# Pair 0's first layer by batches and in an order of its own, the last pair's gates by halves, the slot rows squared on VectorE

## The reference

```python
xn = _layernorm(x)
s = _L0_attn_ref(xn, ...)      # s = xn Wspin + b; e = s WJ; P = softmax(e s^T / sqrt(128))
                               # tanh(beta * (s + mean(s) Wglobal + P s))
g = _silu(_L0_ffn_ref(xn, ...))  # r = sigmoid(xr Wr); k = relu(xk Wk)^2; r * (k Wv); xr, xk mix each token with the one before
x = x + s * g
xn = _layernorm(x)
s = _L1_attn_ref(xn, ...)      # 16-head retention with decay mask, |scores| denominators, RMS norm, gate, Wo
g = _silu(_L1_ffn_ref(xn, ...))  # soft mixture of 8 experts with 64 slots each; slot rows are RMS-normalised once
x = x + s * g
```

## Time and profile before

| what | us |
|---|---|
| median of 3 runs | 1065.32 (1065.32 to 1065.45) |
| the profiled execution, its own time | 1065.09 |
| its span | 1063.3 |
| TensorE busy | 1046.6 (98%) |
| VectorE busy | 918.8 (86%) |
| ScalarE busy | 810.7 (76%) |
| GpSimd busy | 414.3 (39%) |
| TensorE busy in the first 32 us | 23.51 |
| TensorE busy from 1052 to 1060.5 us | 5.86 |

### The profile page before, as it was taken

How to read it: one execution, slowest core, us unless ns; L and a number is a source line. 1 busy time by engine, 2 the same in 40 slices (tenths; PEclk the granted TensorE clock), 3 DMA queues, 4 the chain that set the end, 5 groups by cost and what they waited for, 6 DMA issues and landing times.

```text
span 1063.3 us, 27317 instructions
## 1 busy us (share of the span) xinstructions
PE 1046.6 (98%) x10266; PEld 824.9 (78%) x10266; DVE 918.8 (86%) x1818; ACT 810.7 (76%) x1434; POOL 414.3 (39%) x555
## 2 busy tenths in 40 slices
PE   7999999999999999999999999999999999999997
PEld 4578787877878778787787878778787787877866
DVE  4888988888998888898888988889988889988775
ACT  4577878778787787877778787886877878787775
POOL 2532434334353433534334443343534325343240
PEclk9999999999999999999999999999999999999999
DMA  6000000000000000000000000000000000000000
GB/s 263 12 11 2 2 22 2 21 2 11 12 2 21 2 15 8 2 21 2 21 2 2 22 2 21 2 11 13 2 21 2 21 2 1 23 1 11 2 12 10
DMA packets 18463, 16.85 MB, mean 16 GB/s; under 512 B 800, under 2 KB 17440, under 8 KB 18080
## 3 DMA queue, kind: packets, MB, share of 16 engines
q1 hardware_dynamic: 18336, 15.12, 4.4%
HBM read 10.93 MB, written 4.19 MB: 14 GB/s over the span
## 4 chain that ended last, share of the span: by engine, by line
PE 94%; DVE 2%; issue 1%; ACT 1%; POOL 0%; DVEq 0%; ACTq 0%; POOLq 0%
PE bank L1031 13%; PE bank L987 11%; PE bank L977 11%; PE bank_s L1008 7%; PE bank L997 6%; PE bank L968 5%; PE bank L938 5%; PE bank L833 3%; PE bank L931 3%; PE bank L864 3%; PE bank L960 3%; PE bank L918 3%; PE bank_s L1011 3%; PE bank L884 3%; PE bank L1038 3%; PE bank L1046 2%
## 5 line engine op out<-in xcount | busy, mean ns | idle before, releaser
L326 POOL TENSOR_TENSOR ret_abs<-ret_abs 128x512 f32<-128x512 f32 x128 | 182.3, 1427 | 250.8 <-ACT ret_abs L479 250.6
L659 DVE TENSOR_TENSOR ret<-bank_s,k_sb 128x1536 f32<-128x1536 f32 x128 | 223.7, 1748 | 29.8 <-PE bank_s L1011 20.2
L479 ACT ACTIVATE ret_abs<-ret 128x1536 f32<-128x1536 f32 x128 | 189.6, 1481 | 26.5 <-DVE ret L659 26.5
L987 PEld LDWEIGHTS bank<-w_sb,hact 128*128 128x128 f32 x1024 | 127.9, 191 | 18.0 <-issue 7.8
L987 PE MATMUL bank<-w_sb,hact 128*128 128x128 f32 x1024 | 138.6, 278 | 0.0
L333 POOL TENSOR_SCALAR dT<-dT,drec 128x256 f32<-128x256 f32 x128 | 67.0, 541 | 170.2 <-DVE drec L723 170.2
L977 PE MATMUL bank<-slotsT,w_sb 128*128 128x128 f32 x1024 | 130.1, 275 | 0.4 <-ACT slotsT L469 0.4
L977 PEld LDWEIGHTS bank<-slotsT,w_sb 128*128 128x128 f32 x1024 | 123.2, 192 | 1.7 <-ACT slotsT L469 0.8
L474 ACT ACTIVATE hact<-hact 128x512 f32<-128x512 f32 x128 | 80.2, 628 | 52.1 <-DVE hact L728 51.7
L1031 PE MATMUL bank<-ret,vrow 128*32 128x256 f32 (+1 forms) x2048 | 108.2, 329 | 0.3 <-POOL ret_abs L326 0.3
L1031 PEld LDWEIGHTS bank<-ret,vrow 128*32 128x32 f32 x2048 | 59.9, 109 | 42.0 <-issue 2.5
(11 more groups left out here) (145 smaller groups left out, 2274.2 us busy)
## 6 DMA issues: line engine op xcount, KB each, us to landing
x_sb<-x SPq DMA_DIRECT2D x16, 256.0 KB, 2.7
w_sb<-w SPq DMA_DIRECT2D x2, 2048.0 KB, 14.0
out<-attn SPq DMA_DIRECT2D x16, 256.0 KB, 2.3
v_sb<-vectors SPq DMA_DIRECT2D x1, 705.0 KB, 7.3
k_sb<-consts SPq DMA_DIRECT2D x1, 538.0 KB, 6.1
w_sb<-weights SPq DMA_DIRECT2D x1, 512.0 KB, 4.4
w_sb<-weights SPq DMA_DIRECT2D x1, 320.0 KB, 3.2
slot_sb<-slot_rows SPq DMA_DIRECT2D x1, 256.0 KB, 3.3
```

The costliest lines, as they stand in the source:

```text
L326: pool.tensor_tensor(both[:, :, P:SEQ], both[:, :, P:SEQ], both[:, :, SEQ:3 * P], ALU.add)\
L479: act.activation(ret_abs[:, q % MR], ret[:, q % MR], ACT.Abs).then_inc(ready["ab"].sem, 1)
L659: dve.tensor_tensor(ret[:, q % MR], bank_s[:, :, 0:3 * P], causal.unsqueeze(1).broadcast_to([P, Q, 3 * P]), ALU.mult)\
L987: ins = pe.matmul(bank[:, i * C:(i + 1) * C], hact[:, i, c], w2_sb[:, e, c], start=(c == 0), stop=(c == HC - 1))
```

## The change

Three things are changed. First, `steps_of` takes the lists `FIRST` and `LAST`: step 0 runs in the order of `FIRST` on TensorE, VectorE and ScalarE, and in the last step the tasks named in `LAST` run behind the others, in its order. Second, in pair 0 the tasks `xnT`, `xnTc`, `s`, `sT`, `e`, `eTc`, `local`, `field`, `sp`, `prod`, `x1`, `xn2T` and `xn2Tc` are cut into one part for each batch, with a semaphore `half[...]` for the first; the second batch's results go to the retention's banks `bank_s`, as does `r`. In the last pair `zt`, `zg`, `sg`, `x2` and the store are cut in the same way. Third, VectorE squares the slot rows with one product and one reduction right behind `xn`, waiting for their own load alone, and scales them right behind `mix`. The fillers behind `slots_across` go from eight to four.

```diff
+FIRST = {
+    "PE": [("xnT", 0), ("s", 0), ("e", 0), ("k", 0), ("score", 0), ("global", 0), ("score", 1), ("r", 0), ("PT", 0),
+           ("srow", 0), ("PT", 1), ("v", 0), ("local", 0)],
+    "DVE": [("stat", 0), ("xn", 0), ("mix", 0), ("gbias", 0), ("smax", 0), ("smax", 1), ("ka", 0), ("srec", 0), ("srowc", 0),
+            ("rv", 0), ("field", 0), ("rvg", 0), ("field", 1), ("prod", 0), ("x1", 0), ("prod", 1), ("x1", 1), ("stat2", 0)],
+    "ACT": [("xnTc", 0), ("sT", 0), ("eTc", 0), ("kr", 0), ("sgT", 0), ("P", 0), ("P", 1), ("PTc", 0), ("PTc", 1), ("tr", 0),
+            ("tv", 0), ("sp", 0)]}
+LAST = {
+    "DVE": [("z", 0), ("gated", 0), ("gated", 1), ("z", 1), ("zg", 0), ("attn", 0), ("sg", 0), ("x2", 0), ("zg", 1),
+            ("attn", 1), ("sg", 1), ("x2", 1)],
+    "PE": [("out", 0), ("o", 0), ("out", 1), ("o", 1)]}
+
+EARLY_BANK = {"xnT": 1, "s": 2, "e": 3, "r": 0, "local": 1}
...
-        slot_sq = dT[:, 0, 0, 0:C]
+        slot_sq = d[:].rearrange("p j s -> p (j s)")[:, 0:4 * C].rearrange("p (j c) -> p j c", j=4)
...
+            def in_order(step):
+                under_way = [(name, k, step - age) for name, k, age in order if 0 <= step - age < pairs]
+                if step == 0 and first:
+                    return [(name, k, 0) for name, k in first]
+                if step == pairs + ages - 1 and last:
+                    return [u for u in under_way if u[0] not in {name for name, _ in last}] + [(*u, pairs - 1) for u in last]
+                return under_way
...
-            sp.dma_start(slot_sb[:], slot_rows).then_inc(loaded.sem, 16)
+            sp.dma_start(slot_sb[:], slot_rows).then_inc(rows_in.sem, 16)
...
-            store(pairs - 1)
-            sp.wait_ge(*stored(pairs - 1))
+            rows = out[bass.ds((pairs - 1) * TOK, TOK), :].rearrange("(j p) c -> p j c", p=P)
+            for b in range(2):
+                sp.wait_ge(*(ready["x2"](pairs - 1) if b else half["x2"](0)))
+                sp.dma_start(rows[:, 2 * b:2 * b + 2], attn[:, 2 * b:2 * b + 2]).then_inc(stored.sem, 16)
+            sp.wait_ge(stored.sem, 16 * (pairs + 1))
...
             def slot_norms():
-                pool.wait_ge(loaded.sem, 64)
...
+            def batches(name, done, p, copy):
+
+                for b in range(2):
+                    act.wait_ge(*(filled if b else half)[name](p))
+                    bank = early_bank(name) if b else banks[BANK[name, 0]][:, 0:SEQ]
+                    copy(b, bank).then_inc((ready if b else half)[done].sem, 1)
...
-            def slot_squares():
-                act.wait_ge(loaded.sem, 64)
-                for j in range(4):
-                    if j:
-                        act.wait_ge(ready["slot_ready"].sem, j)
-                    act.activation(slot_sq, slot_sb[:, j], ACT.Square, accum_out=slot_n[:, 0, j:j + 1])\
-                        .then_inc(ready["slot_ready" if j < 3 else "slot_sqs"].sem, 1)
...
+            def slot_squares():
+                dve.wait_ge(rows_in.sem, 16)
+                dve.tensor_tensor(slot_sq, slot_sb[:], slot_sb[:], ALU.mult).then_inc(ready["slot_sq"].sem, 1)
+                dve.wait_ge(*ready["slot_sq"](0))
+                dve.tensor_reduce(slot_n[:, 0], slot_sq, X, ALU.add).then_inc(ready["slot_sqs"].sem, 1)
...
+            def turn_batches(bank, other, src, name):
+                for b in range(2):
+                    pe.wait_ge(*(ready if b else half)[name](0))
+                    for i in range(2):
+                        ins = pe.transpose((bank, other)[b][:, i * P:(i + 1) * P], src[:, 2 * b + i], ident)
+                    ins.then_inc((filled if b else half)[name + "T"].sem, 1)
...
             def s(p, par, k):
+                if p == 0:
+                    for b, bank in enumerate((claim("s", p), early_bank("s"))):
+                        pe.wait_ge(*(ready if b else half)["xnTc"](p))
+                        pe.matmul(bank[:, 0:SEQ], W["spin"], xnT[:, b, 1:SEQ + 1], start=True, stop=True)\
+                          .then_inc((filled if b else half)["s"].sem, 1)
+                    return
...
-                turn_over(8)
+                turn_over(4)
...
```

More of the change, by code:

```diff
@@ L216, in build @@
             ("eoc", E // 2), ("crec", 2), ("z", 2), ("zt", 1), ("zg", 1), ("sg", 1), ("x2", 1))}
+        half = {name: signal(f"half_{name}") for name in (
+            "xn", "xnT", "xnTc", "s", "sT", "e", "eTc", "local", "field", "sp", "prod", "x1", "xn2", "xn2T", "zt", "zg", "sg", "x2")}
         passed = {name: signal(f"passed_{name}") for name in ("vector", "gpsimd")}
@@ L224, in since, with steps_of @@
                 eng.wait_ge(*signal(p, k))
-        def steps_of(tasks, order, between=()):
-            for step in range(pairs + ages):
-                for name, k, age in order:
-                    p = step - age
-                    if 0 <= p < pairs:
-                        tasks[name](p, p % 2, k)
-                        if p == 0 and (name, k) in between:
-                            between[name, k]()
+        def steps_of(tasks, order, first=(), last=(), between=()):
+            def in_order(step):
[5 more added lines that the diff above has]
+                return under_way
+            for step in range(pairs + ages):
+                for name, k, p in in_order(step):
+                    tasks[name](p, p % 2, k)
+                    if p == 0 and (name, k) in between:
+                        between[name, k]()
         block = ctx.enter_context(nc.Block())
@@ L384, in eTc @@
             def eTc(p, par, k):
+                if p == 0:
+                    batches("e", "eTc", p, lambda b, bank: act.activation(eT[:, b * SEQ:(b + 1) * SEQ], bank, ACT.Copy))
+                    return
                 bank = bank_of("e", p)
@@ L424, in xn2Tc @@
             def xn2Tc(p, par, k):
+                if p == 0:
+                    for b in range(2):
+                        act.wait_ge(*(filled if b else half)["xn2T"](p))
+                        bank = early_bank("xnT") if b else banks[BANK["xn2T", 0]][:, 0:SEQ]
+                        ins = act.activation(xn2T[:, b], bank, ACT.Copy)
+                    ins.then_inc(ready["xn2Tc"].sem, 1)
+                    return
                 bank = bank_of("xn2T", p)
@@ L551, in xn_ @@
                                             ALU.subtract, ALU.mult)
+                    if p == 0 and j == 1:
+                        ins.then_inc(half["xn"].sem, 1)
                 ins.then_inc(ready["xn"].sem, 1)
@@ L583, in field @@
             def field(p, par, k):
+                if p == 0:
+                    dve.wait_ge(*ready["srowc"](p))
+                    dve.wait_ge(*ready["srec"](p))
+                    dve.wait_ge(*(filled if k else half)["local"](p))
+                    bank = bank_s[:, EARLY_BANK["local"]] if k else banks[BANK["local", 0]]
+                    for i in range(2):
+                        j = 2 * k + i
+                        ins = dve.scalar_tensor_tensor(out=spin[:, j], in0=bank[:, i * P:(i + 1) * P], scalar=srec[:, j:j + 1],
+                                                       in1=srow[:, j], op0=ALU.mult, op1=ALU.add)
+                    ins.then_inc((ready if k else half)["field"].sem, 1)
+                    return
                 bank = bank_of("local", p)
@@ L850, in e @@
             def e(p, par, k):
+                if p == 0:
+                    for b, bank in enumerate((claim("e", p), early_bank("e"))):
+                        pe.wait_ge(*(ready if b else half)["sT"](p))
+                        pe.matmul(bank[:, 0:SEQ], W["J"], sT[:, b], start=True, stop=True)\
+                          .then_inc((filled if b else half)["e"].sem, 1)
+                    return
                 pe.wait_ge(*ready["sT"](p))
@@ L859, in score @@
             def score(p, par, b):
-                pe.wait_ge(*ready["eTc"](p))
+                pe.wait_ge(*(half if p == 0 and b == 0 else ready)["eTc"](p))
                 bank = claim("score", p, b)
@@ L878, in local @@
                 pe.wait_ge(*ready["srowc"](p))
-                pe.wait_ge(*ready["PTc"](p, 1))
+                if p:
+                    pe.wait_ge(*ready["PTc"](p, 1))
                 bank = claim("local", p)
@@ L882, in local @@
                     b, i = divmod(j, 2)
+                    if p == 0 and i == 0:
+                        pe.wait_ge(*ready["PTc"](p, b))
+                    to = early_bank("local")[:, i * P:(i + 1) * P] if p == 0 and b else bank[:, j * P:(j + 1) * P]
                     for m in range(2):
-                        ins = pe.matmul(bank[:, j * P:(j + 1) * P], probT[:, b, m, i * P:(i + 1) * P], srow[:, 2 * b + m],
+                        ins = pe.matmul(to, probT[:, b, m, i * P:(i + 1) * P], srow[:, 2 * b + m],
                                         start=(m == 0), stop=(m == 1))
+                    if p == 0 and j == 1:
+                        ins.then_inc(half["local"].sem, 1)
                 ins.then_inc(filled["local"].sem, 1)
@@ L889, in r @@
```

(5 more changed lines are left out.)

89 lines of the change are left out of this document (64 added, 25 removed).

## The result

The change takes 1068.11 us in the median of 11 runs (1067.38 to 1069.33), the kernel before 1065.40 (1065.19 to 1067.07); the ratio is 1.0024, with a 95% interval of 1.0015 to 1.0033. That is 2.7 us slower, just beyond the 0.2% that a measurement here can tell, and just above the forecast's range. The profiled execution took 1068.29, its span 1066.5.

A forecast was written before the change was run, and what follows sets the result against it. TensorE, busy 98% of the span, bounds the kernel, so only its two ends can move. 1065.09 less 0.8 (start) plus 1.5 (end) gives 1065.8; the median lies 0.23 higher, so 1066.0 us, range 1064.2 to 1067.9.

The forecast's parts named there:

- The start: Pair 0, up to `xn3T` and `qk`: batch halves make both 0.8 us earlier, though `v` still waits for `tr`.
- The end: Last pair: second `out` waits behind the first `o`, `x2` 1.9 us late, split store saves 0.4; net cost 1.5.
- The squares: Start: the slot rows' product and reduction fit in VectorE's idle 3.08 us ahead of `mix`, costed at nothing.
- The clock: Rival, between the layers: fewer fillers let TensorE's clock fall, costing 1.0 to 2.5 us, 1067.0 to 1068.5; chance 0.25.
- The sum: Whole kernel: 1065.09 less 0.8 at the start plus 1.5 at the end gives 1065.8; median 1066.0 us.
- the like stop ahead of `v`: TensorE's stop at 16.6 to 19.7 us, where the clock might also fall, with smaller loss.
- The end was not free: Rival, last pair: `rs` comes early enough, `o` fits and the end costs nothing, 1064.1 us; chance 0.12.
- The start could not give more: Rival, pair 0: `tr` unhindered or `v` off the chain, start gains 1.2 to 1.7 us, 1065.1 to 1065.6; chance 0.08.

The follow-up runs named there:

- first experiment: The change with six fillers behind the slot rows' transposes in place of four: median 1068.13 us, its profiled execution 1065.84.
- version with fillers at three places: The change with one filler ahead of `v`, six in place of four, and one between `xn2T` and `xn3T`: 1065.99 us, ratio 1.0001.
- best version: The change with `tr` between the two `PTc`, TensorE's old order at the end, six fillers and one ahead of `qk`: 1062.43 us, ratio 0.9970.

## Why the prediction was wrong

**The start: held.** In the full-clock execution with six fillers `v` starts at 19.77 (19.75 forecast), waiting for `tr` as the cyclic list demands; `xn3T` at 31.17 (31.1). The start gives 0.75 (0.8). In the profiled execution of the change it gives nothing, because the opening fillers took 5.49 and `xnT` began at 8.02, where the forecast took over the place of the earlier trace rows. The forecast has no term for that: the same opening fillers took 4.37 in the profile of before and 4.84 in that of the first experiment, where `xnT` began at 7.42. The 5.49 is not the change's doing, since the kernel before with the squares alone shows it too. Whether the split into batches makes the start more exposed to it, no run separates.

**The end: held.** TensorE's stop ahead of the first `o` is 1.32 (1.5 forecast), `x2` is 1.93 late (1.9), the store gives 0.5 (0.4); in all 1.43 (1.5). The run with the old end measured it as 1.3. One sum in it is written wrong: the chain behind the second `out` has two pitches of 0.34 in its first group and not three, which with a tail of 0.42 gives the 3.8 that is stated (3.79 in the profile, 1060.47 to 1064.26); as written it would be 4.1.

**The squares: held.** Moved alone they leave the time where it was, as far as a measurement can tell.

**The clock: the step that failed.** The sum puts the loss of the clock between the layers at nothing. I named it as a rival, priced it at 1.0 to 2.5 and gave it 0.25, and put against it that "the first 32 us hold gaps too, and show no half clock". It came in all eleven runs of the change: their mean clock is 0.998 or less, and the lowest time, 1067.38, lies above the highest, 1066.72, of the version with fillers at three places. One fall costs 1.6 (1068.29 less 1066.72, profiles that began alike), the medians differ by 2.1 (1068.11 less 1065.99). The argument fails twice. It read one execution of the kernel before, and 24 of 105 of its executions are longer by some 1.5, at a lower mean clock where that is known. And it compared the length of single gaps, while TensorE's work over the whole stretch ahead of `qk` had gone down, as the change's window from 28.00 and this one of the kernel before show:

```profile
28.00:32.00 4.00, 2.46 (x10) 0.95 (x9) 3.00 (x13) 0.60 (x1) 2.46 (x5) 1.00 0.03 8
```

That is 2.46 of 4.0 us busy before and 1.06 of 4.2 in the change. The rest of the sum was right: with the clock held by added fillers the change measures 1065.99, where 1066.0 was forecast, and its full-clock execution with six fillers 1065.84, where the sum for a profiled one gave 1065.8. That the median agrees to 0.01 is luck: the runs fall into a lower group of six and an upper one of five, and 1065.99 is the highest of the six; with one run more in the upper group the median would have been 1066.3. The rival's own price, 1067.0 to 1068.5, holds the measured 1068.11; the error was to take it for the less likely case. For the like stop ahead of `v` the forecast said a smaller loss; where the clock fell there it cost the same 1.6.

**The other rivals.** The end was not free. The start could not give more with `tr` behind both `PTc`; with `tr` between them it gives 1.5 more, which the forecast had named as what would be needed. The whole gain of the start is then 2.3 (`xn3T` at 29.66 against 31.92), above the 1.2 to 1.7 that the forecast gave this rival.

**Open.** What share of the change's eleven runs fell ahead of `v`, ahead of `qk` or at both isn't known, as one of them was profiled. The clock figures only say that five of them lost more than the profiled one. Six fillers without the one ahead of `qk` lose the clock in ten of eleven runs of the change, in six of eleven with a filler ahead of `v` too, and in one of six in the best version. The profiled executions of the latter two show the same stops ahead of `qk` (0.57 or 0.56, then 1.48), so whether they truly differ, with six runs on one side, and why, stays unsettled. So does what decides between two executions with the same work and the same stops.

## What to carry to other kernels

Filler matmuls that nobody waits for are still part of the kernel: taking some away, or moving work so that TensorE stands still more, can halve its clock at the start of the next dense stretch, on the critical path, and only windows of the granted clock over a few microseconds, and the times and mean clocks of many runs side by side, show it. In an in-order queue, an operation that waits for a late result must not stand ahead of work that is ready; splitting in halves pays only with that order right. A wait that a general rule adds for a buffer that this step doesn't use can eat a gain made upstream.
